# One list of steps for all five engines of a decoder layer, in place of three stages run side by side

## The reference

```python
def _L0_attn_ref(x, Wk, bk, Wv, bv, Wq, bq):          # "Fourier" part
    k = jnp.fft.fft(x @ Wk.T + bk); v = jnp.fft.fft(x @ Wv.T + bv); q = jnp.fft.fft(x @ Wq.T + bq)
    queried = jnp.cumsum(k * v, axis=1) * jnp.conj(q)
    nrm = jnp.sqrt(jnp.sum(jnp.abs(queried) ** 2, axis=-1, keepdims=True))
    return jnp.real(jnp.fft.ifft(queried / (1e-09 + nrm))) / np.sqrt(d)
...
# cross attention: 16 heads of 64, causal mask, alibi slopes, softmax, output projection
logits = jnp.einsum('bhqd,bhkd->bhqk', q, k) / jnp.sqrt(jnp.float32(Kd)) + causal + alibi
attn = jnp.einsum('bhqk,bhkd->bhqd', jax.nn.softmax(logits, axis=-1), v)
...
def kmoe(x_flat, W_router, A, B, scale, bias, ...):   # 64 experts, 2 of them for each token
    vals, idx = jax.lax.top_k(x_flat @ W_router.T, top_k)
    probs = jax.nn.softmax(vals, axis=-1)
    Y = jnp.einsum('nkoi,nij,nkpj->nkop', A[idx], xs, B[idx])
    return jnp.einsum('nkop,nk->nop', Y, probs).reshape(...) * scale + bias
...
x = x + _L0_attn_ref(_layernorm(x), ...)
x = x + _L0_xattn_ref(_layernorm(x), ctx_1024, ctx_1024, ...)
x = x + _L0_ffn_ref(_layernorm(x), ...)               # kmoe up, exact gelu, kmoe down
```

## Time and profile before

| | |
|---|---|
| median of 3 runs | 2094.16 us (2092.22 to 2102.57) |
| profiled execution, its own time | 2100.63 us |
| its span, first to last instruction | 2098.9 us |
| busy: PE, DVE, ACT, POOL | 1786.7, 977.7, 862.8, 673.8 us |
| mean granted TensorE clock | 0.861 |

### The profile page before, as it was taken

One profiled execution on the slowest core, in us unless ns is written; L12 is line 12 of the kernel. 1 busy time (PEld: TensorE's weight loads), 2 busy tenths in 40 slices (PEclk: granted clock), 3 DMA queues, 4 the chain that ended last, 5 costly groups with the idle time before them and its releaser, 6 DMA issues. The chain is left out here.

```text
span 2098.9 us, 51180 instructions
## 1 busy us (share of the span) xinstructions
PE 1786.7 (85%) x17202; PEld 1389.5 (66%) x17202; DVE 977.7 (47%) x3954; ACT 862.8 (41%) x2550; POOL 673.8 (32%) x2386
## 2 busy tenths in 40 slices
PE   6888979788897988979799897988979889897866
PEld 5676757667675776757667676775757667575644
DVE  2345354543545455354543545455354543545543
ACT  2443445343543444444443443434444443443421
POOL 3104242332423234241332423224231342423332
PEclk9998979889797998979889797998979889797866
DMA  8000000000000000000000000000000000000000
GB/s 232 11 6 6 2 11 7 12 6 12 2 7 11 7 11 7 2 11 7 12 6 12 1 7 12 7 12 6 2 11 7 12 6 9 4 2 7 2 6 7
DMA packets 18582, 27.25 MB, mean 13 GB/s; under 512 B 2193, under 2 KB 17170, under 8 KB 18066
## 3 DMA queue, kind: packets, MB, share of 16 engines
q1 hardware_dynamic: 18322, 23.98, 3.8%
HBM read 19.78 MB, written 4.19 MB: 11 GB/s over the span
## 5 line engine op out<-in xcount | busy, mean ns | idle before, releaser
L346 POOL COPY chosen_dn<-experts 64x64 f32 x1024 | 196.2, 249 | 612.8 <-issue 530.8
L333 POOL COPY chosen_up<-experts 32x128 f32 x1024 | 290.3, 308 | 249.9 <-PE G L838 105.4
L970 DVE CUSTOM_DVE_ANT_0 probs<-S,distance 128x128 f32<-128x128 f32 (+1 forms) x512 | 152.7, 353 | 134.3 <-PE S L720 133.3
L557 ACT ACTIVATE probs<-probs,neg_max 128x128 f32<-128x128 f32 (+1 forms) x512 | 190.7, 443 | 42.2 <-DVE neg_max L970 40.8
L333 ACT COPY chosen_up<-experts 32x128 f32 x512 | 123.3, 292 | 137.5 <-PE G L838 127.3
L749 PE MATMUL X<-vals,probsT 128*128 128x65 f32 x512 | 111.1, 301 | 79.0 <-issue 78.3
L838 PE MATMUL G<-chosen_up,W 128*64 128x256 f32 x1024 | 169.3, 460 | 6.0 <-DVE W L1076 6.0
L749 PEld LDWEIGHTS X<-vals,probsT 128*128 128x128 f32 x512 | 84.6, 207 | 110.4 <-issue 109.3
L824 PE MATMUL F<-chosen_up,own 64*64 64x128 f32 x1024 | 100.4, 323 | 64.7 <-POOL chosen_up L333 62.6
L672 PE MATMUL P<-ctxT,wk 128*128 128x256 f32 x512 | 153.8, 453 | 0.0
L529 ACT ACTIVATE kT<-P,bk 128x256 f32<-128x256 f32 x128 | 53.7, 470 | 241.8 <-PE P L672 241.8
(11 more groups left out here) (129 smaller groups left out, 3382.7 us busy)
## 6 DMA issues: line engine op xcount, KB each, us to landing
x<-in_x SPq DMA_DIRECT2D x16, 256.0 KB, 2.7
ctxT<-in_ctxT SPq DMA_DIRECT2D x16, 256.0 KB, 2.7
out<-x2b SPq DMA_DIRECT2D x16, 256.0 KB, 2.2
r_dn<-in_r_dn SPq DMA_DIRECT2D x1, 2048.0 KB, 15.6
experts<-in_experts_up SPq DMA_DIRECT2D x2, 1024.0 KB, 22.4
wk<-in_xWk SPq DMA_DIRECT2D x1, 1024.0 KB
wo<-in_xWo SPq DMA_DIRECT2D x1, 1024.0 KB
wv<-in_xWv SPq DMA_DIRECT2D x1, 1024.0 KB, 7.7
```

The lines of the kernel that those rows point to most:

```text
L333: last = copy(dst, src.rearrange("p (m c) -> p m c", m=2))
L346: last = copy(dst, src.rearrange("p (m c) -> p m c", m=2))
L557: act.activation(probs[e % 4][:, lo:hi], probs[e % 4][:, lo:hi], ACT.Exp, bias=neg_max[:, e % 4, rt:rt + 1], scale=-1.0).then_inc(probs_re ...
L970: dve.tensor_tensor_reduce(probs[e % 4][:, lo:hi], S[e % 2][:, lo:hi], distance[:, (1 - rt) * P:2 * P], SLOPES[e], TOP, ALU.add, ALU.min, ...
```

## The change

The list is now a table, ORDER, of 298 words `step.index@lag`: in turn t a step with lag L works on batch t - L. So each step chooses its batch for itself. Five projections (v.2, v.3, q.2, q.3, k.3) get lag 1, the first scores of a batch (`score.0`, `score.1` with `mask` and `exp.0`) get lag 0, and the third layernorm and `logits_up` with `top_up` and `gap_up` get lag 1; a turn begins at `spread_up`. There are still 18 turns and 14 of them have all three batches. Each engine's choices have a name of their own (`choose_pool`, `choose_dve`, `choose_act`). Users of P0 and P1 alternate in the list's order, and the waits on P, F and G are counts in that order (`p_bank`, `take_p`, `take_f`, `take_g`). The small routing tables exist once for each of the two layers, and the product W has a buffer of its own for the second layer. The extra semaphore increment `hold` after many waits is gone.

```diff
-def hold(eng, passed, sem, value):
-    eng.wait_ge(sem, value)
-    eng.sem_inc(passed, 1)
+def after(eng, sem, value):
+    if value > 0:
+        eng.wait_ge(sem, value)
...
+ORDER = """
+x1_bias@1 load_x x2_bias@2 v.2@1 weights_up@2 ln1_stats turn_a.0@1 catch_a.0@1 spread_up@2 keep_up@2 v_keep.2@1 q.2@1
...
 def steps_in_order():
...
+    for word in ORDER.split():
+        step, _, lag = word.partition("@")
+        name, _, n = step.partition(".")
+        order.append((name, int(n) if n else None, int(lag or 0)))
+    last = max(lag for _, _, lag in order)
+    for turn in range(BATCH + last):
+        for name, n, lag in order:
+            if 0 <= turn - lag < BATCH:
+                yield name, n, turn - lag
+
+def run(steps):
+    for name, n, b in steps_in_order():
+        if name in steps:
+            if n is None:
+                steps[name](b)
+            else:
+                steps[name](b, n)
+
+def turns_of(users):
+    turns = {}
+    for name, n, b in steps_in_order():
+        if name in users:
+            turns[name, n, b] = len(turns)
+    return turns
...
-        W = [sb("W0", [P, A_DN]), sb("W1", [P, A_DN // 2])]
+        W_up, W_dn = [sb("W0", [P, 2 * B_UP]), sb("W1", [P, 2 * B_UP])], sb("W_dn", [P, A_DN])
+        pm = [sb("pm_up", [P, UP_GROUPS * TOPK]), sb("pm_dn", [P, TOKENS])]
+        offsets = [sb(f"offsets{i}", [1, TOKENS * TOPK], I32) for i in (0, 1)]
...
+        def p_bank(name, n, b):
+            turn, which = divmod(p_turns[name, n, b], 2)
+            return (P0, P1)[which], p_kept[which], turn
...
             def k_proj(f, r):
-                to = (P0, P1, P1, P1)[r]
+                bank = take_p("k", r, f)
                 if r == 0:
                     pe.wait_ge(ctx_loaded, at(f, 16, 16))
-                    pe.wait_ge(f_kept, at(f, 6, 4))
-                else:
-                    pe.wait_ge(v_kept, at(f, 4, r))
...
+            def take_g(name, n, c):
+                after(pe, g_kept, g_turns[name, n, c])
...
             def first(c, v):
+                take_f("first", v, c)
...
-                hold(pe, passed, chosen_pool, at(c, GROUPS, 2 * v + 2))
+                for name in CHOOSERS:
+                    pe.wait_ge(chosen[name][0], at(c, UP_GROUPS, 2 * v + 2))
...
             def bias_x2(c):
-                pool.wait_ge(result_free, at(c, 1, 1))
+                after(pool, out_stored, at(c, 16, 0))
```

More of the change, by code:

```diff
@@ new lines @@
+turn_b.1@1 catch_b.1@1 first.0@2 weigh.0@2 mask.3@1 second.0@2 choose_dve.2@2 choose_dve.3@2 choose_dve.4@2 f.1
+f_keep.1 choose_act.3@2 turn_a.2@1 choose_pool.2@2 choose_pool.3@2 choose_pool.4@2 cross.0 pre.0@2 k.3@1
+choose_pool.5@2 choose_dve.5@2 first.1@2 pv.1@1 weigh.1@2 k_keep.3@1 f.2 product_kv choose_act.4@2 choose_act.5@2
+choose_act.6@2 second.1@2 catch_a.2@1 pre.1@2 exp.3@1 f_keep.2 score.4@1 norm.1@1 first.2@2 lane.0 choose_dve.6@2
+choose_dve.7@2 load_ctx choose_pool.6@2 choose_pool.7@2 weigh.2@2 choose_pool.8@2 second.2@2 k.0 turn_b.2@1
@@ new lines @@
+choose_dve.8@2 choose_act.7@2 pre.2@2 cumulate choose_dve.9@2 catch_b.2@1 keep.1@1 cross.1 choose_dve.10@2
+choose_pool.9@2 choose_act.8@2 k.1 first.3@2 weigh.3@2 k_keep.0 choose_act.9@2 choose_act.10@2 product_q lane.1
+choose_pool.10@2 second.3@2 choose_pool.11@2 keep_out.1@1 v.0 v_keep.0 pre.3@2 choose_dve.11@2 choose_act.11@2
+first.4@2 k_keep.1 mask.4@1 choose_act.12@2 weigh.4@2 choose_dve.12@2 pv.2@1 norm.2@1 turn_a.3@1 second.4@2
+choose_dve.13@2 catch_a.3@1 score.5@1 pre.4@2 first.5@2 choose_pool.12@2 weigh.5@2 choose_dve.14@2 turn_b.3@1 keep.2@1
@@ new lines @@
+keep_out.2@1 exp.4@1 catch_b.3@1 Q choose_pool.13@2 choose_act.13@2 choose_act.14@2 second.5@2 pre.5@2 mask.5@1 pv.3@1
+turn_a.4@1 catch_a.4@1 choose_pool.14@2 inverse norm.3@1 first.6@2 power weigh.6@2 choose_act.15@2 choose_dve.15@2
+keep.3@1 turn_b.4@1 second.6@2 pre.6@2 choose_pool.15@2 first.7@2 weigh.7@2 exp.5@1 keep_out.3@1 score.6@1 second.7@2
+pre.7@2 v.1 catch_b.4@1 turn_a.5@1 pv.4@1 mask.6@1 root x1.0 ln2_stats.0 x1.1 ln2_stats.1 gelu@2 exp.6@1 catch_a.5@1
+score.7@1 norm.4@1 router_dn@2 logits_dn.0@2 v_keep.1 ln2_root turn_b.5@1 logits_dn.1@2 keep.4@1 logits_dn.2@2
@@ L72, in steps_in_order @@
+q_keep.1 top_up@1 gap_up@1
+"""
+P_USERS = ("turn1", "f", "inverse", "turn2", "k", "v", "q")
+F_USERS = ("ln3_turn", "first", "dn_first", "y_turn")
+G_USERS = ("logits_up", "spread_up", "second", "router_dn", "spread_dn", "dn_second", "y_turn")
 def steps_in_order():
     order = []
[L76 to L131, removed]
-        else:
-            steps[name](which, n)
@@ L546, in power @@
+                last.then_inc(kept, 1)
             def power(f):
+                bank, _, _ = p_bank("inverse", None, f)
                 act.wait_ge(inverse_done, at(f, 1, 1))
```

553 lines of the change are left out of this document (281 added, 272 removed).

## The result

The changed kernel takes 1746.87 us, the median of four runs (1744.98 to 1750.27), against 2096.97 (2092.22 to 2102.57) for the kernel before on the same chip: a ratio of 0.833, 95% interval 0.830 to 0.836.

What follows compares the result with a forecast made beforehand. PE, busy 85%, was taken as the bound. Fourteen turns of 107.6 us (97.2 work, 5.8 waits, 4 clock, 0.6 unseen waits), ends 325.5 and 1.7 around the span gave 1834, as a median 1828; range 1760 to 1925.

Steps and rivals of the forecast that it cites:

- (1): PE waits at second.0, .2 and .3, which follow their first at once: 2.1 us a turn in all.
- (2): PE waits at dn_second.0, .2 and .3, which follow their dn_first at once: 2.35 us a turn in all.
- (3): y_turn waits for bank F, held by the copy of layernorm 3, with one score as cover: 0.35 us a turn.
- (4): logits_up waits for bank G, which final frees, near the turn's end: 0.95 us a turn.
- The clock of a full turn: Four waits clustered at the turn's end set off some 8 us at half clock, 4 us lost a turn.
- Rival A: Full clock kept everywhere: a turn of 103.0 us, median 1764 us; chance 0.10.
- the place that I took as a model: End of a turn before: waits of 0.79 and 0.94 in the cluster behind which half clock set in at 1024.
- The ends: First two and last two turns, 330.5 us before: 5 us less, between -20 and +15, so 325.5.
- B: The clock doesn't recover and its 13.0 us a turn stay: turn 116.0, median 1945 us; chance 0.10.
- C: Another engine, POOL or ACT, is late by 2 to 4 us a turn: median 1870 us; chance 0.15.
- D: Slower: bare second steps keep PE at 1.2 GHz from first.0 to second.7, 2330 us in all; chance 0.02.
- E: The order hardly matters, as other waits replace the removed ones: 2060 to 2100 us; chance 0.03.

Runs made afterwards that it cites:

- tail_two_short: Changed kernel with one DVE product of unused output ahead of the weighing of dn_second.2 and of dn_second.3; 1795 us, one run.
- hold_in_after: Changed kernel with the removed semaphore increments put back behind the waits where the kernel before had them; 1766.7 us.
- no_hold_pe: Kernel before without the semaphore increments behind its holds on PE only, 14 a batch; 2094.8 us, ratio 0.999.
- no_hold: Kernel before without the semaphore increment behind each hold, nothing else; 2035.4 us, ratio 0.969.
- ln3_late: Changed kernel with layernorm 3, its transposes, logits_up and the search for the largest logits back at the start of the next turn; 1884.9 us.
- mid_one: Changed kernel with four DVE products of unused output ahead of the weighing of second.6, in the middle of a turn; 1819 us, one run.

## Why the prediction came out as it did

**The turn at the full clock: right.** The prediction's sum was 97.2 of work and 5.75 of waits, 103.0. Measured: 96.5 and 6.1. The listed waits in the profiled turn: (1) `second` 0.62 + 0.98 + 0.62 against 0.6 + 0.95 + 0.55; (2) `dn_second` 0.52 + 0.88 + 0.88 against 0.6 + 0.85 + 0.9; (3) 0.28 against 0.35; (4) 1.05 against 0.95. Only the 0.73 ahead of the spreading was missed. Each came from a bare chain of before plus what stood in the queue ahead of it.

**The clock of a full turn: the step that failed.** "I take one or two short stretches, some 8 us at the half clock, full of work, which is 4 us lost". The place was right: four of the five half stretches that are left stand behind the cluster at the turn's end. The size was not: some 3.4 us in five turns of fourteen, 0.6 us a turn in place of 4. These 3.4, and the 1.0 by which work and all waits were less (96.5 + 6.1 against 97.2 + 5.8 + the 0.6 for waits not seen), make 1506 - 1445 = 61 of the 89 us missed (1834 against 1745.4 for the profiled execution). Rival A, to which I gave 0.10, is what happened in the turns. The runs show how near the edge that was. With 1.6 us more of waiting in the same cluster (tail_two_short) the clock costs 2.0 a turn, with 2.2 to 2.6 more 3.5 to 3.9. My 4 would have been right with waits two us longer.

The likely reason lies in the rows of before around the place that I took as a model. The 0.94 was DVE's; PE's own waits there were 0.79 and 0.78, and the half clock set in at 1024.0, right behind them. The long waits for layernorm 3 come after that:

```profile
1023.42 0.21 PE L882 MATMUL F<-ident,experts 32*128 32x32 f32 x1 [0.78 <-DVE experts L1103]
...
1028.37 1.11 PE L778 MATMUL F<-ident,xn 128*128 128x128 f32 x4 [2.68 <-DVE xn L910]
1030.73 0.69 PE L643 MATMUL P<-ident,xn 128*128 128x128 f32 x2 [1.25 <-DVE xn L910]
```

So small waits alone did set off the half clock, as I said, and then it held for 10.2 us with 3.9 us of idle inside. In the new turn what stands behind the cluster is full of work, and each of the four stretches is over after 3.4 us. I had priced the new stretch by the old one's length. Why it sets in behind some borders of turns and not behind the others was not tested.

**The ends: the second step that failed.** "I take -5, between -20 and +15". Measured: 298.3 against 330.5, so -32. Split as above by idle time, the ends have 73.4 us idle now and 84.8 before, 11.4 less. The other 21 are busy time that fell with the same work in it: at the half clock the last stretch had 65 us before and 38 after. I let cover fill idle time there, but kept the ends' clock. In the last stretch this is partly luck: it has 33 to 39 us idle in every kernel, and with the same order of steps it took 77.5 in the changed kernel and 86.5 in hold_in_after, as it took 85.9 in the kernel before and 79.2 in no_hold_pe. The Trainium skill ("TensorE: Matmul & The Clock Gate", section "What's actually happening") says that the number of matmuls at the low clock varies with the phase in which a kernel meets the clock gate; the spread of 7 and 9 us here would fit that, but no run varied the phase alone. From one execution to the next a kernel's whole time moved by 5 (changed), 8 (hold_in_after), 10 (before) and 13 us (no_hold_pe).

**The hold increments: wrong for the old list, harmless for the sum.** I priced them at zero as standing "on engines that PE does not wait for". The earlier trace rows already had PE waiting for POOL, 4.1 us a turn, and PE did wait for the increments: they cost 62 us before and 20 in the new list, where half of the 20 is in the ends. The sum was made for a turn without them, so no term moved. But as an account of the gain it was wrong, since 62 of the 350 us need no new list at all.

**What should have shown:** in the full turns the transposes of layernorm 3 find their data ready, `pv` waits 1.7 us in the whole run, DVE and ACT are as before, and PE is busy 94% of a turn. The waits of 0.5 to 1.05 are eight and not six, and the granted clock is 0.99 and not 0.96. POOL is at 655, not within 1% of 674. Its choices are shorter, 297 ns against 308 by the groups' means; it is not the increments (307 in no_hold), and the cause was not tested. `gelu`'s switch stayed hidden, as forecast. Rivals B, C, D and E are out: the clock recovered, a full turn waits for nothing but the forecast chains and the 0.7 at the spreading, and the order matters by 296 us.

**What stays open:** which engine's increments cost the 62 us, and at what mix of idle and busy the clock falls. The runs bracket it but don't give a law.

## What to carry to other kernels

When PE is the bound and its clock varies, sum a turn as work at the full clock, plus waits, plus clock, and bracket the clock with doses: lengthen one wait by a known amount, in the very place, and see what the clock adds. There is no one slope. Here an us of added wait at the turn's end cost 0.9 to 1.5 us more by the clock (1.4 for 1.6, 2.9 for 2.6, 3.3 for 2.2), 0.7 in the middle of a turn (1.8 for 2.5), and 0.4 where one wait of 7.1 covered much of the half stretch itself (2.7 for 6.7, ln3_late). What a half stretch costs is half of the work that falls into it, so ask what stands behind the waits, and not only how long they are. Instructions that do nothing but count (a semaphore increment behind a wait) are worth taking out by themselves first: one line less, 129 increments a batch, gave 3%. A sum of the new order, chain by chain, was good to 1 us in 103.

## What the hardware showed that I had not expected

One or two semaphore increments between two choices lengthen POOL's pause by 0.16 us, and 14 a batch on PE cost nothing that can be measured (0.999, 0.997 to 1.000). DVE's `ln3` takes 2.72 us beside POOL's bias sums and 0.73 without them. The granted clock falls while PE idles, not only behind the wait: in mid_one the half stretch begins at 719.0, inside the wait of 2.70 that ends at 719.94.

```profile
719.94 1.97 PE L839 MATMUL G<-chosen_up,W 128*64 128x256 f32 x8 [2.70 <-DVE W L1087]
```

And eight waits of 0.5 to 1.05 us in a turn of 103 leave the clock alone in nine turns of fourteen.
